# Diagonal 64-token blocks in the attention stage, and k's part of the difference by per-tile scalar operations

## The reference

```
x = x + xattn(layernorm(x), ctx, ctx, ...)
x = x + ffn(layernorm(x), weight, bias)

# in xattn, q and k being [128, 64, 128]:
q_prob, k_prob = prob(q), prob(k)       # tanh(x)*0.499+0.5, divided by its row sum
log_ratio = log(q_prob) - log(k_prob)
sid  = einsum('bnd,bmd->bnm', q_prob - k_prob, log_ratio)
attn = softmax(-sid / D**0.5, axis=-1)
attn_feat = einsum('bnm,bmd->bnd', attn, v)
f_diff = (v - attn_feat) @ W_diff.T + b_diff + q
h   = layernorm(f_diff, ln_g, ln_b)
out = gelu(h @ W1.T + b1) @ W2.T + b2 + f_diff      # and a last layernorm
```

## Time and profile before

| | us |
|---|---|
| median of 3 runs | 280.61 |
| lowest, highest | 280.08, 280.77 |
| the profiled execution's own time | 280.14 |
| its span, first to last instruction | 278.2 |
| PE, DVE, ACT, POOL busy in the span | 214.7, 230.7, 211.6, 161.1 |

### The profile page before, as it was taken

The page is one execution under the profiler, slowest core; times in us unless marked ns, Lnnn a source line. Parts: engine busy times, 40 slices in busy tenths (PEclk is TensorE's granted clock), DMA queues, the critical chain, the costliest instruction groups (busy, mean ns, idle before and its releaser), DMA issues.

```text
span 278.2 us, 5345 instructions
## 1 busy us (share of the span) xinstructions
PE 214.7 (77%) x1511; PEld 186.8 (67%) x1511; DVE 230.7 (83%) x860; ACT 211.6 (76%) x747; POOL 161.1 (58%) x172
## 2 busy tenths in 40 slices
PE   2668556661798778877589999999999999999230
PEld 1556444451687667765579999999999999998110
DVE  2779999989799999999832778888888988889961
ACT  4599999995599999999776665777777777777520
POOL 2476766667566545658064357666677776665540
PEclk9998999985599999999999999999999999999855
DMA  5855555500000000000019336687777777774677
GB/s 148 243 162 153 176 157 157 160 4 1 1 0 0 2 0 5 0 0 0 2 16 101 38 39 78 75 114 110 104 105 102 108 91 103 99 100 77 123 107 148
DMA packets 44765, 22.30 MB, mean 80 GB/s; under 512 B 2240, under 2 KB 44608, under 8 KB 44736
## 3 DMA queue, kind: packets, MB, share of 16 engines
q0 software_dynamic: 16896, 8.39, 26.6%
q1 hardware_dynamic: 27408, 13.38, 17.7%
q10 hardware_dynamic: 432, 0.20, 0.4%
HBM read 9.37 MB, written 4.19 MB: 49 GB/s over the span
## 4 chain that ended last, share of the span: by engine, by line
PE 43%; DVE 27%; ACT 16%; DMA 6%; issue 3%; POOL 3%; SPq 0%; DVEq 0%; POOLq 0%; ACTq 0%
PE bank L889 20%; DVE q_c L673 9%; DVE LN_c L681 6%; DVE F L696 6%; PE bank L879 5%; ACT TQK L421 5%; PE bank L880 5%; PE bank L881 5%; ACT TQK L437 5%; DMA LN_c<-in_ctx_dram 5%; PE bank L909 2%; ACT PV L432 2%; ACT vT_c L426 2%; DMA F<-rows 2%; PE bank L802 1%
## 5 line engine op out<-in xcount | busy, mean ns | idle before, releaser
L889 PE MATMUL bank<-W2T,TQK 128*128 128x128 f32 x512 | 68.0, 279 | 0.0
L889 PEld LDWEIGHTS bank<-W2T,TQK 128*128 128x128 f32 x512 | 64.5, 191 | 4.1
L517 ACT ACTIVATE TQK<-bank,b1c 128x512 f32<-128x512 f32 x64 | 43.9, 687 | 24.5 <-PE bank L881 24.4
L340 POOL TENSOR_TENSOR q_c<-TQK,GAINK 128x512 f32<-128x512 f32 x16 | 19.6, 1225 | 23.8 <-PE bank L854 23.3
L879 PE MATMUL bank<-hTh,W1h 128*128 128x512 f32 x64 | 29.2, 456 | 1.7 <-DVE hTl L769 1.7
L319 POOL TENSOR_TENSOR xrstd<-xvar,pow_c 128x4 f32<-128x4 f32 x16 | 16.8, 1051 | 22.1 <-DVE xvar L601 22.1
L383 POOL TENSOR_TENSOR ovar<-sso,eps_c 128x4 f32<-128x4 f32 x16 | 3.1, 192 | 44.6 <-ACT TQK L531 44.6
L673 DVE SCALAR_TENSOR_TENSOR q_c<-TQK,GAINQ,q_c 128x128 f32<-128x128 f32 x64 | 26.9, 480 | 2.1 <-POOL q_c L343 2.0
L880 PE MATMUL bank<-hTl,W1h 128*128 128x512 f32 x64 | 25.4, 396 | 0.0
L881 PE MATMUL bank<-hTh,W1l 128*128 128x512 f32 x64 | 25.2, 394 | 0.0
L715 DVE TENSOR_TENSOR F<-bank,F 128x512 f32<-128x512 f32 x16 | 11.1, 691 | 16.9 <-PE bank L889 13.2
(11 more groups left out here) (121 smaller groups left out, 659.3 us busy)
## 6 DMA issues: line engine op xcount, KB each, us to landing
F<-rows POOLq DMA_DIRECT2D x32, 256.0 KB, 5.1
LN_c<-in_ctx_dram SPq DMA_DIRECT2D x16, 256.0 KB, 3.0
X<-in_x_dram SPq DMA_DIRECT2D x16, 256.0 KB, 3.4
out_dram<-F SPq DMA_DIRECT2D x16, 256.0 KB, 4.2
LN_c<-in_L_xattn_W_dram SPq DMA_DIRECT2D x1, 256.0 KB, 6.3
lT_c<-in_L_xattn_W_dram SPq DMA_DIRECT2D x1, 256.0 KB, 4.7
E_c<-in_L_xattn_W_diff_dram ACTq DMA_DIRECT2D x1, 64.0 KB, 2.7
rows<-in_L_xattn_b_diff_dram ACTq DMA_DIRECT2D x1, 64.0 KB, 4.6
```

Of the source, the lines that this page charges most:

```text
L517: act.activation(buf(hid_c, m, HB * C)[:, j * C:(j + 1) * C], M1_B[j % 2][:, :], ACT.Gelu, bias=b1c[:, j:j + 1]).then_inc(gelu_ready, 1)
L889: last = pe.matmul(M2_B[m.buf][:, i * D:(i + 1) * D], buf(hid_c, m, HB * C)[:, j * C + i * D:j * C + (i + 1) * D], W2T[:, j * D:(j + 1) * ...
```

## The change

It has three parts, all in the second stage.

1. Scores: in place of one 128x128x128 product for each tile, two products with 64 stationary columns and 64 moving columns each, one for each diagonal block. They are written side by side, so that a chunk's scores are 128 partitions by 256 columns.
2. Exponentials and weighted sum: one exponential instruction over 128x256 in place of two over 64x256. The weighted sum of a tile becomes two products that use 64 rows (partitions 0 to 63, or 64 to 127) and 64 stationary columns each, with 129 moving columns as before. The memset of E_c and its semaphore go; ACT waits for `sel_ready`, an old event, in its place.
3. k's part on POOL: four operations of 128x128 that multiply by a per-row factor and add a per-row shift in one go, in place of the two of 128x512.

```
-                if is_chunk(k, 2):
-                    pool.wait_ge(w_ps, 1)
-                    pool.wait_ge(sel_ready, 1)
-                    pool.memset(E_c[:, :], 0.0).then_inc(e_zero, 1)
...
-                    pool.tensor_tensor(tiles(buf(diff_c, k)), tiles(chunk(TK, k)),
-                                       over_features(per_tile(GAINK, k)), ALU.mult).then_inc(kscaled, 1)
-                    pool.wait_ge(kscaled, k.n + 1)
-                    pool.tensor_tensor(tiles(buf(diff_c, k)), tiles(buf(diff_c, k)),
-                                       over_features(per_tile(SHIFT, k)), ALU.add).then_inc(kpart, 1)
+                    for i in range(G):
+                        last = pool.tensor_scalar(tile(diff_c, k, i), all_tile(TK, k, i), per_tile(GAINK, k, i, 1),
+                                                  per_tile(SHIFT, k, i, 1), ALU.mult, ALU.add)
+                    last.then_inc(kpart, 1)
...
-                    for h in range(2):
-                        rows_h = slice(h * S, (h + 1) * S)
-                        last = act.activation(tiles(buf(E_c, k))[rows_h, :, rows_h],
-                                              tiles(S_B[k.buf][:, :])[rows_h, :, rows_h],
-                                              ACT.Exp, scale=-float(D) ** -0.5)
-                    last.then_inc(e_ready, 1)
+                    act.activation(buf(E_c, k, G * S), S_B[k.buf][:, 0:G * S], ACT.Exp,
+                                   scale=-float(D) ** -0.5).then_inc(e_ready, 1)
...
-            act.wait_ge(e_zero, 1)
+            act.wait_ge(sel_ready, 1)
...
-                        last = pe.matmul(EP_B[k.buf][i // 2][:, o:o + D + 1], tile(E_c, k, i),
-                                         all_tile(PV, k, i, D + 1, D + 1), start=True, stop=True)
+                        for b in range(2):
+                            rows_b = slice(b * S, (b + 1) * S)
+                            last = pe.matmul(EP_B[k.buf][i // 2][rows_b, o:o + D + 1],
+                                             buf(E_c, k, G * S)[rows_b, i * S:(i + 1) * S],
+                                             all_tile(PV, k, i, D + 1, D + 1)[rows_b, :], start=True, stop=True)
...
-                        last = pe.matmul(S_B[k.buf][:, i * D:(i + 1) * D], tile(lT_c, k, i), tile(dT_c, k, i),
-                                         start=True, stop=True)
+                        for b in range(2):
+                            rows_b = slice(b * S, (b + 1) * S)
+                            last = pe.matmul(S_B[k.buf][rows_b, i * S:(i + 1) * S], tile(lT_c, k, i)[:, rows_b],
+                                             tile(dT_c, k, i)[:, rows_b], start=True, stop=True)
```

More of the change, by code:

```diff
@@ L223, in xattn_ffn_kernel @@
             sem("rows_ready"), sem("wd_ps"), sem("wd_sb"), sem("w_ps"), sem("w_sb"))
-        b1_ps, w_done, wf_step, wf_q, wf_ps, wf_sb, e_zero = (
+        b1_ps, w_done, wf_step, wf_q, wf_ps, wf_sb = (
             sem("b1_ps"), sem("w_done"), sem("wf_step"), sem("wf_q"), sem("wf_ps"), sem("wf_sb"),
-            sem("e_zero"))
+            )
         b2_added = [sem(f"b2_added{i}") for i in range(3)]
@@ L238, in xattn_ffn_kernel @@
         norm_step, halfk_ready, norms, lratio = sem("norm_step"), sem("halfk_ready"), sem("norms"), sem("lratio")
-        kscaled = sem("kscaled")
         kpart, ln_ready, diff_ready, lr_ready = sem("kpart"), sem("ln_ready"), sem("diff_ready"), sem("lr_ready")
```

## The result

The changed kernel takes 271.22 us (270.51 to 271.67, 4 runs) against 280.69 of the kernel before in the same comparison: ratio 0.9665, 95% interval 0.9638 to 0.9691, so 9.5 us less. The profiled execution's span went from 278.2 to 268.5 us.

The account below looks back on a forecast made before the run. A DVE-POOL ring of 4.00 us per chunk bounded the second stage, ACT within hundredths. Start -2.0, twelve chunks -5.6, end -0.5, in all -8.1: 280.14 to 272.0, stated as 272.3 us for the runs' median; range 270.0 to 280.5.

Parts of the forecast that it names:

- a ring of DVE and POOL: Second stage, before the change: DVE and POOL exclude each other over SBUF, 1.91 plus 2.09, 4.00 us per chunk.
- The twelve chunks: Second stage, chunk 0 to chunk 12: 4.07 us each before, 3.60 after, so -5.6 us.
- the exponential: On ACT: two exponentials of 0.78 us by starts become one of 0.39.
- The forecast's bound (ACT): Second stage after the change: ACT sets the pace at 3.60 us per chunk, with DVE below it at 3.5.
- the idle time that I named as a sign: Sign of a right forecast: DVE has some idle time before L673 or L681.
- POOL's part: Four small operations take 1.2 to 2.3 us per chunk and hold DVE 0.04 to 0.1 each; 2.09 of exclusion goes.
- The low case: PE's step per chunk in the second stage: the halves overlap or nearly so, 2.7 to 3.4 us.
- The threshold of 0.088: Microseconds per small PE instruction at which PE's step reaches 4.0 us; rival that small products are dear, 15%.
- the halves don't overlap: Rival, 22%: PE's step is 3.7 to 4.1 us and PE the bound; 275.5 us, from 274 to 279.
- The start: Start of the second stage: L610 and L620 no longer held up by POOL, chunk 2's operations earlier; -2.0 us.
- The end: End of the second stage: last exponentials -0.39, last weighted sum 0 to +0.9, POOL's weight operations still collide; -0.5 us.
- The memset: 0.95 us of POOL at 20 us, off the chain: worth 0.

Follow-up runs that it names:

- POOL's part alone: The kernel before with only k's four multiply-and-add operations on POOL in place of the two of 128x512: 276.09 us, ratio 0.9822.
- the blocks alone: The changed kernel with POOL's two operations of 128x512 put back, so only scores, exponentials and weighted sum are changed: 279.88 us, ratio 0.9971.
- three squares: The changed kernel with the squares of one tile in four left out on ACT: 270.29 us, ratio 0.9646.
- the copy: The changed kernel with one more POOL operation per chunk, a one-input copy of 128x512 to a scratch area: 276.56 us, ratio 0.9838.
- the constant multiplication: The changed kernel with one more POOL operation per chunk, a one-input multiplication by a constant over 128x256: 272.58 us, ratio 0.9722.
- the run with the loops exchanged: The changed kernel with all four products of one half before those of the other, in weighted sum and scores: 271.44 us, ratio 0.9672.
- the run with one subtraction: The changed kernel with DVE's four log-ratio operations replaced by one subtraction over 128x512, leaving out the per-row term LRATIO: 268.24 us, ratio 0.9559.

## Why the prediction was right, step by step

**What bounded the kernel** was read rightly: a ring of DVE and POOL at 4.00 us with ACT some hundredths behind. POOL's part alone gave ACT's figure, 3.96 against the forecast's 3.97 to 4.00; the blocks alone left the ring in place. The pieces that I gave the ring were not the right ones, though. That 1.91 and 2.09 add to 4.00 proves nothing, as any cut of one period does. POOL's pair doesn't start when L681 is through: L340 starts at 123.48, 0.18 before that, released by L854. By the releases in the earlier trace rows the ring is: from L343's end (121.75) to L854's start behind the last L673 0.99, to L854's end (123.40) 0.66, to L340's start 0.08, and the pair 2.27: 4.00. L681 runs beside it. The exclusion is one link, the wait of POOL for PE's transposes another.

**The twelve chunks** were put at -5.6 and gave -6.5. The term that was mis-sized is the exponential: 0.39 by starts was read from two instructions on 64 partitions, and the one on 128 takes 0.26. With a few hundredths from the copies and the squares, ACT's work is therefore 3.43 and not 3.60. The forecast's bound (ACT) held, but DVE stands at the same figure, so it has none of the idle time that I named as a sign, and a further 0.1 off ACT would have brought nothing: with POOL's operations beside it DVE's sum is 3.44, where I took 3.5. That -5.6 came so near was also luck. Twelve chunks at 3.44 would have given -7.6. But the first four steps took 3.50 to 3.61 each and the one from chunk 11 to 12 took 4.01, where POOL's weight operations begin, which costs 1.0 together. I had priced all twelve chunks alike, and the two errors partly cancel.

**POOL's part.** Four operations of the slower form, 0.43 by starts each, 1.89 in all, inside the 1.2 to 2.3 that were given. They cost DVE 0.04 in total as L369 had suggested. This holds for the arrangement that the changed kernel settled in: with three squares the same four cost 0.18. The reason is better known now. If DVE's operation arrives while POOL's is under way, it waits. If POOL's arrives while DVE's four are running, POOL's waits, and DVE loses 0.03. The Trainium skill, SBUF — State Buffer, section Who interferes with whom, calls the shared ports an exclusive lock; that they are held for the whole instruction it says of DVE's two-port modes. The runs agree that the two engines exclude each other and that one of them stands still: DVE's operation ended 0.14 after POOL's beside L343, the copy, and the last small one where that had come first. For the constant multiplication they don't agree on the length (0.14 held of 0.87, and DVE's operation ended first).

**PE's part.** The low case was taken and holds: 1.10 and 0.69 us for a chunk, by starts 1.04 and 0.61, so 0.065 and 0.038 per small instruction. The threshold of 0.088 was far off. The reason given (overlap) is what the starts show. The rival "the halves don't overlap" isn't settled as a time, since the run with the loops exchanged keeps a part of the overlap; the estimate above, 3.7 us for the step, is the low end of what the rival had. The 0.12 that I charged for each small instruction of the weighted sum was near: one alone takes 0.11.

**The start** was put at -2.0 and gave -2.8. L610 and L620 (now L600 and L610) shrank as predicted, from 0.88 and 0.94 to 0.09 and 0.10, and the first difference of chunk 2 was gone from the chain. The chain of the changed kernel there:

```profile
66.30 0.09 DVE NORM L600
...
67.28 0.10 DVE SHIFT L610
...
67.41 0.31 DVE q_c L663
...
68.75 1.09 PE bank L849 x4
69.84 1.03 PE bank L854 x4
...
70.89 0.61 ACT lT_c L476
...
71.64 1.12 PE bank L841 x16
72.76 1.05 PE bank L849 x4
73.80 0.85 PE bank L854 x4
74.66 1.94 PE bank L829 x16
...
76.62 0.25 DVE nrden L680 x2
```

It runs through PE, as I had argued when I counted 2 and not 3; its weighted sum there takes 1.94 at the lower granted clock, against 1.10 later. When the clock comes back differs between executions, and the mark moves with it. In the run with three squares, whose products and start are those of the changed kernel, the weighted sum of chunk 0 took 1.15 and the mark stands at 75.99, 0.9 earlier. The table of stretches, the changed kernel first, then that run:

```profile
74.60:76.60 2.00, 2.00 (x19) 1.66 (x20) 0.08 (x1) 1.63 (x2) 1.53 (x4) 0.50 0.00 0
74.60:76.60 2.00, 2.00 (x36) 1.76 (x37) 0.85 (x5) 1.88 (x3) 1.40 (x4) 0.97 0.00 0
```

The run with POOL's part alone, with the old products, has 1.00 there and the same mark, 75.99. So that the start gave 2.8 and not 3.7 is no price of the new products; it is the granted clock of that execution.

**The end** was put at -0.5 and gave -0.2. The last exponential is 0.37 instead of 0.75, the last weighted sum 1.10 instead of 1.16, but POOL's thirteen weight operations still collide with DVE: the run with one subtraction, where DVE has idle time, passes the same chunks 1.6 us faster.

**The memset** was forecast to be worth nothing. No run removed it alone; in the run with the blocks alone, which has no memset either, the mark of chunk 0 is not earlier (80.11 against 79.71).

**The addition** itself has a slip: 272.0 and 0.5 are 272.5, and 272.3 was said.

## What to carry to other kernels

Add up an engine's work by differences of starts, over one period, for every engine, before pricing a change: here two bounds stood 0.04 us apart, and parts that bring 5.0 and 0.8 us alone bring 9.4 together. An operation that is longer than its twins of the same form is a wait in disguise; look for what ended just before it did. Where two engines exclude each other, look at who comes first: the same POOL operations cost DVE 0.04 in one arrangement and 0.18 in another. And idle time on an engine (PE was busy 28.86 of 34.00 us) hides much of what an elegant overlap on it saves, so size the slack first.

## What the runs showed of the hardware

- An exponential over 128x256 occupied ACT for 0.26 us, and one over 64x256 for 0.39, with a strided pattern or a contiguous one. The instructions themselves lasted 0.36 to 0.38; the next one started later behind those on 64 partitions.
- Float32 products on 64 rows and 64 columns, 129 moving columns: one instruction every 0.11 us on the same diagonal block, and two every 0.11 with the other block next to it (1.04 us for 16). With 128 rows, 64 stationary and 64 moving columns, 16 took 0.61 by starts side by side and 0.90 half after half. The switches between these shapes and the full array, three times per period, left no gap over 0.17 us that a wait doesn't explain.
- A POOL operation that had begun held DVE's two-input operation: 0.60 us beside the two-input one of 1.04 (128x512), 0.35 beside the copy of 0.66 (128x512), 0.18 beside the multiply-and-add of 0.44 (128x128), and in these three DVE's ended 0.14 after POOL's. It was 0.14 beside the constant multiplication of 0.87 (128x256), where DVE's ended first.
- The other way round, a multiply-and-add of POOL that arrived while DVE's four were running lasted 0.60 in place of 0.45 and cost DVE 0.03.
- The granted clock came back to 1.00 at different times in executions with the same start: in 74.60 to 76.60 it was 0.50 in one and 0.97 in the other, and the mark of chunk 0 lay 0.9 us apart.
